# VectorE's maximum of the scores placed between the second and third tile of the second combination, in the fusing stage of a gated cross-attention block

## The reference

```
x = x + tanh(g_ffn[0]) * moe(layernorm(x))           # top 2 of 8 experts, and 2 shared ones
s = einsum('bsd,bvd->bsv', layernorm(x), ctx)        # ctx: 8 x 77 x 512
x = x + tanh(g_xattn[1]) * einsum('bsv,bvd->bsd', softmax(s), ctx)
x = x + tanh(g_ffn[1]) * conv_ffn(layernorm(x))      # inputs rounded to 8 bits, by a scale per token
```

## Time and profile before

| | |
|---|---|
| runs | 1667.28, 1670.91, 1675.32 us, median 1670.91 |
| the profiled execution | 1673.33 us, its span 1671.7 us |
| mean granted TensorE clock | 0.935 of full |
| TensorE busy | 1510.4 us, 90% of the span |
| VectorE busy | 1053.8 us, 63% |
| ScalarE busy | 815.9 us, 49% |
| GpSimd busy | 743.7 us, 44% |
| fuse, stages 0 to 7 | about 1130 to 1287 us of the span |

### The profile page before, as it was taken

The page is one execution under the profiler, slowest core; times in us unless marked ns, Lnnn a source line. Parts: engine busy times, 40 slices in busy tenths (PEclk is TensorE's granted clock), DMA queues, the critical chain, the costliest instruction groups (busy, mean ns, idle before and its releaser), DMA issues. The chain is left out here.

```text
span 1671.7 us, 24835 instructions
## 1 busy us (share of the span) xinstructions
PE 1510.4 (90%) x8764; PEld 1147.7 (69%) x8764; DVE 1053.8 (63%) x1759; ACT 815.9 (49%) x1448; POOL 743.7 (44%) x666
## 2 busy tenths in 40 slices
PE   6589999999978999989999999988888789999997
PEld 5478788788756888867787788765554455555553
DVE  3468878788728564332332333247996899999995
ACT  2145555555522221213343444325777778888883
POOL 0044344435414675243414100255551878888870
PEclk9789999999978999999999999995766889999998
DMA  3157656666326999735535333459772111111112
GB/s 142 46 182 252 210 207 252 228 212 230 127 85 216 355 356 345 247 120 176 179 105 169 119 107 107 138 145 319 235 258 92 38 39 38 64 63 63 52 51 101
DMA packets 131428, 270.31 MB, mean 162 GB/s; under 512 B 16083, under 2 KB 31443, under 8 KB 129288
## 3 DMA queue, kind: packets, MB, share of 16 engines
q1 hardware_dynamic: 100168, 175.47, 31.2%
q0 software_dynamic: 16624, 62.93, 10.7%
q10 hardware_dynamic: 14544, 30.68, 4.9%
HBM read 145.56 MB, written 122.42 MB: 160 GB/s over the span
## 5 line engine op out<-in xcount | busy, mean ns | idle before, releaser
L243 PE MATMUL e_u_ps<-e_xs,w_shared 128*128 128x512 f32 x720 | 169.4, 396 | 6.4 <-DVE e_sg L1262 6.4
L243 PEld LDWEIGHTS e_u_ps<-e_xs,w_shared 128*128 128x128 f32 x720 | 137.6, 192 | 35.4 <-DVE e_sg L1262 6.5
L2357 PE MATMUL f_banks<-b_xdT,w1h 128*128 128x512 f32 x512 | 146.0, 427 | 14.5 <-POOL b_xdT L2107 9.7
L2133 POOL TENSOR_TENSOR b_h<-b_h,b_srow 128x512 f32<-128x512 f32 x112 | 143.3, 1333 | 26.3 <-ACT b_srow L2169 26.3
L1458 PE MATMUL e_u_ps<-e_w,e_xs 128*128 128x512 f32 x528 | 133.0, 401 | 2.0 <-DVE e_xs L1354 1.2
L2357 PEld LDWEIGHTS f_banks<-b_xdT,w1h 128*128 128x128 f32 x512 | 97.1, 196 | 48.2 <-POOL b_xdT L2107 14.1
L2326 PE MATMUL b_o_ps<-w2q,b_h 128*128 128x512 bf16 x448 | 116.9, 384 | 8.7 <-ACT b_h L2163 8.7
L2158 ACT ACTIVATE b_h<-b_h 128x512 f32<-128x512 f32 x128 | 88.2, 690 | 53.4 <-DVE b_h L2248 52.4
L1362 DVE TENSOR_TENSOR e_hT<-e_r_ps,e_hT 128x256 fp32r<-128x256 f32 x69 | 29.3, 424 | 134.5 <-ACT e_hT L1200 134.5
L1458 PEld LDWEIGHTS e_u_ps<-e_w,e_xs 128*128 128x128 f32 x528 | 95.7, 188 | 23.2 <-DVE e_xs L1354 1.6
L2245 DVE SCALAR_TENSOR_TENSOR b_h<-f_banks,cw,b_h 128x511 f32<-128x511 f32 x128 | 95.2, 744 | 22.1 <-ACT b_h L2152 22.1
(11 more groups left out here) (267 smaller groups left out, 3504.5 us busy)
## 6 DMA issues: line engine op xcount, KB each, us to landing
slots_in_scratch<-e_xs SPq DMA_DIRECT2D x22, 1024.0 KB, 8.3
e_xe<-slots_in_scratch SPq DMA_DIRECT2D x69, 256.0 KB, 2.7
experts_out_scratch<-e_ye ACTq DMA_DIRECT2D x69, 256.0 KB, 2.0
yx_a<-in_w POOLq DMA_DIRECT2D x10, 1024.0 KB, 5.9
xin<-in_x SPq DMA_DIRECT2D x16, 512.0 KB, 5.0
xres<-in_x SPq DMA_DIRECT2D x16, 512.0 KB, 5.3
x_scratch<-x SPq DMA_DIRECT2D x32, 256.0 KB, 3.4
xn_scratch<-xn SPq DMA_DIRECT2D x32, 256.0 KB, 2.0
```

Of the source, the lines that this page charges most:

```text
L243: mm = pe.matmul(n.u_ps[:, (2 * q + j) % 4], ws[q // n.KH][:, pa, at:at + P], xs[:, pb, k], start=(k == 0 and (pa, pb) == PASSES[0]), stop ...
L2133: pool.tensor_tensor(ht, ht, srow[:], ALU.mult).then_inc(u_done, 1)
L2357: mm = pe.matmul(f_ps[:, v % RING], n.w1h[:, k, (c - NV) * P:(c - NV + 1) * P], xdT[:, part, k], start=(k == 0 and part == 0), stop=(k == ...
```

## The change

VectorE's second combination is given the tiles that it works on. Where it was called once for all four tiles ahead of the maximum of the scores, it is now called for tiles 0 and 1 ahead of it and for tiles 2 and 3 behind it. Nothing else differs; the waits and counts of every other engine are the same.

```diff
-            def combine_second(s, o):
+            def combine_second(s, o, tiles):
 
-                for j in range(TB):
+                for j in tiles:
                     dve.wait_ge(comb, (s + 1) * 2 * TB + j + 1)
                     dve.scalar_tensor_tensor(out=x1[o][:, j], in0=y2[o][:, j], scalar=gcol[:, o, 1, j:j + 1],
                                              in1=y1[o][:, j], op0=ALU.mult, op1=ALU.add).then_inc(comb, 1)
...
                 if front:
-                    combine_second(s, o)
+                    combine_second(s, o, (0, 1))
                 if mid:
                     dve.wait_ge(s_full, s + 1)
                     dve.tensor_reduce(nm[:], s_ps[:, :, 0:C], AX.X, ALU.max, negate=True).then_inc(nm_done, 1)
+                if front:
+                    combine_second(s, o, (2, 3))
                 if back:
                     for j in range(TB):
                         dve.wait_ge(x4_done, (s - 1) * TB + j + 1)
```

## The result

The changed kernel took 1679.26 us in the median of five runs (1677.26 to 1679.36), the kernel before 1670.8 in five runs. The ratio is 1.0039 with an interval of 1.0021 to 1.0058: slower by some 6.5 us (the two medians alone lie 8.5 apart), within the 0.5% that I called no change, though the interval reaches 0.58%. The profiled execution has a span of 1677.6 us against 1671.7, with 24835 instructions in both. One execution of a later run, prt_early_third, took 2118.06 us at a granted clock of 0.655, and its ratio leaves that one out.

The account below looks back on a forecast made before the run. In the fusing block VectorE and TensorE both had little room, so the order of waits decides. Stage costs 0 + 0 + 0.7 + 1.2 + 0.1 + 0 + 0.5 = 2.5 us on 1670.91 gave 1673.4 us, range 1667 to 1679.

Parts of the forecast that it names:

- The forecast of the stretch: Fusing block: from stage 0's score end to stage 7's it takes 139.3 us instead of 136.8.
- stages 3 and 4: VectorE's delay reaches TensorE's third product whole in stage 3, cost 1.2 us; stage 4, TensorE late itself, 0.1 us.
- rival 1: Fusing block: nothing remains, as an earlier clock rise gives back costs of 0.7 and 1.2 us; 1670.9 us, chance 0.20.
- The gain costed at nothing: Stages 1 to 6: maximum comes forward 3.7 us in all, worth nothing because ScalarE's normalisations cover it.
- The bound of -3.7: Lower bound of the sum: the maximum's whole forward move is gained, -3.7 us, 1667.2 us.
- The sign that I gave: ScalarE: the first exponential still starts within 0.1 us of the last normalisation's end.
- Stage 0: Two combinations, 1.37 us, move behind an existing wait, hidden by the first output tile's 2.40 us wait for TensorE.
- Stages 1 and 2: GpSimd waits of 1.83 and 1.13 us swallow delays 0.87 and 1.07; cost 0, and 0.7 through stage 2's third product.
- Rival 2: Fusing block: exponentials were held by the maximum, so up to 3.7 us are gained; 1667.2 us, chance 0.08.
- Rival 3: New TensorE pauses keep the clock down through the scores in three stages, 12.4 us; 1683.3, chance 0.08 with rival 4.
- Rival 4: Maximum hardly comes forward, delaying VectorE 1.37 us in seven stages, 9.6 us; 1680.5, chance 0.08 together with rival 3.
- The FIFO rule: VectorE's and ScalarE's queues are strict FIFO; by that alone the cost is every wait, 3.95 us.

Follow-up runs that it names:

- prt_early_third: Changed kernel with the ScalarE queue of prt_early and VectorE's maximum between the third and fourth tile; ratio 1.0038.
- null: The kernel before, unchanged, timed against itself; ratio 1.0011.
- again: The changed kernel, unchanged, timed once more against the kernel before; ratio 1.0024.
- max_third: Changed kernel with the maximum moved between the third and fourth tile of the second combination; ratio 0.9999.
- max_first: Changed kernel with the maximum ahead of all four tiles of the second combination in stages 0 to 6; ratio 1.0066.
- delay_only: Kernel before plus one combination of 0.74 us, its result unread, behind the maximum in stages 0 to 6; ratio 1.0009.
- delay_two: Kernel before plus two combinations, 1.46 us, results unread, behind the maximum in stages 0 to 6; ratio 1.0045.
- prt_early: Changed kernel with ScalarE reordered: two normalisations, exponentials, third normalisation, copy prT, fourth normalisation, then the next block's copies; ratio 1.0023.
- two_early: As prt_early_third, with VectorE's first two x3 tiles also ahead of the next element's statistics; ratio 1.0233.
- x3_early: Changed kernel with VectorE's scale rt and first x3 tile ahead of the next element's statistics; ratio 1.0068.

## Why the prediction was right, and where its sizes were not

**The direction and the place** were right: nothing gained, a wait of VectorE for the scores in stages 1 to 4 and 6 and none in 5 (0.43 us there in the second profile), and it passes on through the first x3 tile to TensorE's third product. The forecast of the stretch, 139.3 us, met the first profile's 139.23, by luck as will be seen; the second had 140.86. With two profiles of each kernel the block lost 3.7 us on average (140.05 less 136.38), not 2.5, and the two ratios give 4.0 and 6.5 us (intervals 1.7 to 6.4 and 3.5 to 9.7; 2.5 lies in the one only). The range of 1667 to 1679 has the second set's time, 1676.59, well inside; the first, 1679.26, is over its upper end by 0.3 us, though the ratio of that set puts the change on the first median at 1670.91 x 1.0039 = 1677.4.

**The step that was too small** was stages 3 and 4. Score end to score end, in both profiles of each kernel (null and again are the second ones):

```
stage      0-1    1-2    2-3    3-4    4-5    5-6    6-7
before   17.82  20.29  20.00  18.68  19.72  20.28  20.01
null     18.18  20.28  18.67  19.74  20.03  20.25  18.81
after    17.60  19.88  20.17  20.42  20.46  20.31  20.39
again    18.08  20.08  20.49  20.64  20.55  20.53  20.49
forecast     0      0   +0.7   +1.2   +0.1      0   +0.5
```

The sum agreed with the first profile because errors cancelled: stages 0 to 2 were taken too high (0.7 in all for -0.5) and stages 3 and 4 too low (1.2 for 1.7, 0.1 for 0.7). The premise behind it was that a shift moves scores and combinations alike and the waits stay as the old trace has them. They did not: they were 0.61, 0.61, 0.43, 0.45, 0 and 0.64 us in the first profile and 1.09, 1.46, 1.00, 0.95, 0.43 and 0.85 in the second, where I had 0.87, 1.07, 1.18, 0.28, 0 and 0.55.

When the maximum starts with the scores, a stage runs in a loop: scores, maximum, first x3 tile, third and fourth product, transposes, scores. From the rows of stage 3 after: 8.46 to the x3 tile, 0.81 to the third product (1207.26), 2.29 to the fourth (1209.55), and from there 8.86 to the next scores' end (1218.41), in all 20.4 us. The old rows give 20.0 for the same loop: 0.04, then 7.53 from the maximum to the tile's end, 1.37, 0.06, 2.29, and 8.66 from 1204.80 to 1213.46; the 0.4 us between the two are not explained. The kernel before has score ends 18.7 us apart (one in the first profile, two in the second, 18.67 and 18.81), the changed one none under 19.8 past the first. I had seen the 18.7 and put it under rival 1.

But 18.7 was never VectorE's own period. From the start of one maximum to the next, the first profile before has 20.09, 19.89, 19.58, 20.09 and 19.64 us between stages 1 and 6, with VectorE busy 17.9 to 18.2 us of each, and the changed kernel 19.89, 20.17, 20.41, 20.46 and 20.31. After the short stage the scores merely lay ready 1.04 us before VectorE came to them. VectorE had little room in any stage, so what it lost was nearly all lost by the kernel: the waits of the maximum in stages 1 to 6 were 0.63, 2.74, 5.78 and 10.94 us in max_third, the changed kernel's two profiles and max_first, and the stretches lie 0.0, 2.9, 4.5 and 9.2 us above the mean of 136.38. The added combinations of delay_only and delay_two, 4.4 and 8.8 us in these six stages, lengthened it by 4.3 and 7.0. That this is the reason for the size fits every such run, but it was reckoned afterwards; no run was made to test it.

**The gain costed at nothing**: right in size, wrong in its reason. I named ScalarE's normalisations as the cover and priced its loss at 3.7 us. prt_early took the cover away and gained nothing; behind it stands the late x3 tile. The bound of -3.7 was no real end of the range. The sign that I gave, exponentials within 0.1 us of the last normalisation's end, failed in stage 2 of the second profile, where ScalarE waited 0.33 us for the maximum and nothing was gained either.

**Stage 0** was hidden as said: its first x3 tile still waited 0.95 us for TensorE (2.40 before), 1.0 having been forecast. **Stages 1 and 2**: in the first profile the bias still waited 0.91 and 0.92 us for GpSimd, so their delays were inside there, as forecast. In stage 2 the fourth product did come later, 11.19 us after the scores' end (1189.01 - 1177.82) for 10.30, but the transposes and scores behind it took 0.72 less, 7.12 us for 7.84. The transposes before and after; the scores behind them took 4.13 and 3.69 us:

```profile
1186.94 3.92 PE L1930 MATMUL f_t_ps<-ident,f_xn 128*128 128x128 f32 x16
```

```profile
1190.87 3.59 PE L1932 MATMUL f_t_ps<-ident,f_xn 128*128 128x128 f32 x16
```

From 4.0 to 3.5 us before the scores' end the granted clock was 0.50 before and 0.99 after: the rise fell earlier against the work. That is the mechanism of rival 1, and in this stage it gave back most of the cost.

**The rivals.** Rival 1 (nothing remains) falls as a whole: the stretches of the two kernels don't overlap. Its mechanism acted in stage 2 of the first profile. Rival 2 falls with prt_early. Rival 3, the clock, did not come true here: after stage 0 the score groups took 3.69 to 3.74 us in the first profile and 3.76 to 4.13 in the second, against 3.69 to 4.13 before. two_early shows that such slow scores exist, at 6.95. Pauses in front of an output product did not bring them, neither 1.9 us ahead of the third in prt_early nor 1.55 ahead of the fourth in x3_early (stage 3 of each, the scores behind them 3.7). In two_early the pauses lie within the transposes, but whether they are the cause stays open: pauses of 2.66 and 0.72 us were followed by scores of 6.95 us at the end of stage 0 and of 4.51 at the end of stage 1. My remark that TensorE pauses most in stage 0 doesn't hold for the window: it was idle 2.62 of 19.00 us there and 4.63 of 20.50 in that of stage 1 at clock 0.67; the longest pause, 5.99 us, lies ahead of stage 0. Rival 4 falls: against the scores the maximum of stages 1 to 6 came forward by 0.4, 0.2, 0.1, 1.0, 1.4 and 0.7 us, as reckoned.

**The FIFO rule** of the Trainium skill, "PSUM — Partial Sum Buffer", "Engine vs sequencer instructions", is borne out: in max_first four ready combinations stand behind a waiting maximum 10.94 us in all. Its price by all waits, 3.95, is nearer to the measured 3.7 than my 2.5. The waits themselves were 2.74 and 5.78, so that 3.95 met their mean of 4.3 is in part luck; that nearly all of each wait was lost is what the four kernels above show.

**Left open**: why delay_only lengthened its profiled stretch by 4.3 us and its timed runs by only 1.5 (no more than 3.7 by the interval; the medians, 1677.10 and 1674.46, lie 2.6 apart). A stretch comes from one execution, and the two of the changed kernel differ by 1.6 us, with the longer scores in the second; more executions were not profiled. No version faster than the kernel before came out; max_third equals it.

## What to carry to other kernels

Moving a consumer earlier in an in-order queue pays only if its data are there before the new slot; otherwise it is a wait in front of ready work. Ask three things of each row: when the data come, what the consumer's own consumer is busy with, and what waits at the end of the queue for the work now displaced. When a change adds a wait in every stage of a pipeline, don't let the slack of single stages swallow it: look for the engine that is busy nearly the whole of every stage, measure its own period from one of its instructions to the same one in the next stage, and count each wait added to it as lost. Two events on another engine can lie closer together in one stage, as the score ends 18.7 us apart did, without that engine having any room.

## What the runs showed of the hardware that was not expected

The same kernel's blocks ahead of the fusing one end up to 4.3 us apart in two executions (1136.67 and 1141.01; over all fourteen profiles, with the same code up to there and on several chips, stage 0's scores end between 1129.13 and 1141.01), and the ratio of the same code to itself in twelve runs was 1.0011 with 1 just inside its interval. A difference of 2 us in this kernel needs the profile of the stage; the time alone does not show it.
